# Attention output with both units of a query block in one PSUM bank, normalised between two 32x32 vector transposes

## The chip, the cores and the metric

One NeuronCore of a Trainium2 chip runs the kernel. The metric is device time in microseconds, the median of several executions. One more execution was taken by the hardware profiler. The engines are PE (matmul), ACT (ScalarE), DVE (VectorE), POOL (GpSimd) and SP (which issues the DMAs).

## The reference

`x` has 2 x 1024 tokens of 128 features in float32. The block is FFN, attention, FFN, each with a residual:

```python
x = x + 0.5 * ffn(layernorm(x))      # 8 dense experts of 256 hidden, weighted by norm_g
x = x + attn(layernorm(x))
x = x + 0.5 * ffn(layernorm(x))

# attn: 8 heads of 8 dimensions
xn = (x - mu) * rsqrt(var + eps) * ln_w + ln_b
q, k, v = split(xn @ w_qkv)          # w_qkv 128 x 192
q, k = l2norm(q), l2norm(k)
sim = where(causal, 8.0 * q @ k.T, min)
o = softmax(sim) @ v                 # [b, h, n, 8] -> [b, n, 64]
out = o @ w_out                      # w_out 64 x 128
```

## The kernel before

Tokens are worked in four groups of 512. Group p is (batch p // 2, query block p % 2). Both FFN layers run as rounds of one hidden chunk of 128: three `up` matmuls (L443, L446, L449), a Gelu on ACT, a split into high and low parts on DVE (L932, L934) and three `down` matmuls (L461, L464, L466). PE works LAG = 3 chunks ahead of `down`. Between the two FFN layers lies the attention.

The attention has eight units, numbered u: (batch, query block, quad), a quad being four of the eight heads. A unit of query block 0 has three quad steps, one of query block 1 has seven; that makes 40 quad steps, and units end with steps 2, 5, 12, 19, 22, 25, 32 and 39. A quad step is two steps s, each for two heads: `scores` (L570) writes 2 x up to 512 columns into one of S_SETS = 3 pairs of PSUM banks, and ACT's Exp (L778) moves them to `probs`. The last quad step of each unit is half as wide (256 columns a head). POOL masks the diagonal ones (L1254). `pv` (L591) multiplies `probs` by `v_ones`, whose rows of 32 hold 8 values of a head, a one (which gives the softmax's denominator) and zeros; it accumulates a unit in one bank, 32 partitions a head. `output_bank(u)` alternates between banks 7 and 6.

PE's order is written out: round k has the two `scores` of quad step k, then `pv(k - 3)`, then at most one job of the list `jobs` whose time is k - 3. A job (`fill`) writes the bank that no unit is using, and DVE empties it (`empty`). PE's fill n waits until job n - 1 is emptied, and the first `pv` of a unit waits until every earlier job is emptied. The jobs of one unit's output are:

- `copy_o` on DVE: bank to `oT` (L1076)
- `rows`: four 128x128 transposes of `oT` (L622); DVE then takes the reciprocal (L1107) and multiplies into `o_tok` (L1109)
- after each second unit `features`: four transposes of `o_tok` (L625), copied to `o_feat` (L1114)
- `project`: four matmuls of `o_feat` (64 rows) with `wout_sb` (L628), added to `x_sb` by DVE (L1118)

Other jobs bring in group 3 (LAST): `ln`, `qk`, `v`, `q_stack`, `k_stack` (transposes of groups 2 and 3), and `ffn_ln`, the first transposes of the second FFN. Those of the last unit (`rows`, `features`, `project`) stand in the first group of the second FFN, after chunks 2, 4 and 6; its `copy_o` is at chunk 0 of DVE.

Of the kernel before, what the change touches and what calls it, by code (L numbers as in the profile page):

```python
# [49 lines left out]
ROW = 32  # L50
SCALE = 8.0
# [45 lines left out]
def build(nc, x, ln_w, ln_b, w_qkv, w_out, gate_w, gate_b, rms_w, w1, b1, w2, b2, out):  # L97
# [9 lines left out]
    with ctx:  # L107
# [26 lines left out]
        wout_sb = sb("wout_sb", [INNER, DIM])  # L134
# [35 lines left out]
        oT = sb("oT", [P, GROUP])  # L170
        rden = sb("rden", [P, GROUP_TILES, 4])
        o_tok = sb("o_tok", [P, GROUP_TILES, INNER])
        o_feat = sb("o_feat", [INNER, GROUP])
# [35 lines left out]
        o_copied, rden_done = sem("o_copied"), sem("rden_done")  # L209
# [15 lines left out]
        for st in steps:  # L225
# [10 lines left out]
        u0, u1, u2, u3 = last_quad[0:4]  # L236
        jobs = [(u0 + 1, "rows", 0), (u0 + 2, "q_stack", LAST - 1), (u0 + 3, "k_stack", LAST - 1),
                (u1 + 1, "rows", 1), (u1 + 2, "features", 1), (u1 + 3, "project", 1),
                (u1 + 4, "ln", LAST), (u1 + 5, "qk", LAST), (u1 + 6, "v", LAST), (u2 + 4, "rows", 2),
                (u2 + 5, "q_stack", LAST), (u2 + 6, "k_stack", LAST)]  # L240
        for u in range(3, len(units) - 1):
            at = last_quad[u] + 1
            jobs.append((at, "rows", u))
            if u % 2:
                jobs += [(at + 1, "features", u), (at + 2, "project", u)]
        jobs.append((last_quad[4] + 2, "ffn_ln", 0))
        jobs.sort(key=lambda j: j[0])
        u = len(units) - 1
        jobs += [(quad_steps, "rows", u), (quad_steps, "features", u), (quad_steps, "project", u)]
        assert len({at for at, *_ in jobs}) == len(jobs) - 2  # L250
        job_number = {(kind, arg): n for n, (_, kind, arg) in enumerate(jobs)}

        def output_bank(u):
            return 7 - u % 2

        def job_bank(n):

            at = jobs[n][0]
            return 13 - output_bank(steps[2 * min(at, quad_steps - 1)]["unit"])
# [23 lines left out]
        def schedule(layer, g):  # L283
            if not isinstance(g, int):
                return AT
            return AT_ZERO if (layer, g) == (0, 0) else AT_LAST if (layer, g) == (0, LAST) else AT_THIRD if (layer, g) == (0, 2) else AT_FIRST if (layer, g) == (1, 0) else AT

# [39 lines left out]
        def unit_vectors(eng, p):  # L327
            if p < LAST:
                eng.wait_ge(qkv_copied, p + 1)
            else:  # L330
                eng.wait_ge(job_emptied, job_number["qk", p] + 1)
# [70 lines left out]
        def _(pe):  # L402
# [194 lines left out]
            def fill(n):  # L597
# [3 lines left out]
                if n:  # L601
                    pe.wait_ge(job_emptied, n)
# [677 lines left out]
```

## Time and profile before

| | us |
|---|---|
| median of 3 runs (298.69 to 298.80) | 298.76 |
| the profiled execution | 298.09 |
| its span, first to last instruction | 296.4 |
| first FFN, in the span | 0 to 118 |
| attention | 118 to 194 |
| second FFN | 194 to 296 |

The rows of the trace are in us from the span's start. PE, ACT, DVE and POOL are busy for 280.2, 226.1, 216.8 and 87.0 us of the span. What lies between the span and the execution's time is 298.09 - 296.4 = 1.69 us.

### The profile page before, as it was taken

Reading aid. Unit: us, or ns where it says so; the run is one execution under the profiler, and the core shown is the slowest. Engines: PE = TensorE matmul, PEld = TensorE weight load, DVE = VectorE, ACT = ScalarE, POOL = GpSimd, SP = SyncE. Lnnn points to the kernel's source line nnn. Section 1 sums busy time; section 2 is a strip of 40 time slices with the busy share of each in tenths; the row PEclk is TensorE's granted clock in tenths of the full one; section 3 lists DMA queues with packets and bytes.
Section 4 is the critical chain, followed back from the end, with each engine's and each line's share of the span. In section 5 each row is a group of like instructions: output and inputs, shape, how many; then the busy total and the mean of one; then the engine's idle time right before and its main releaser. Section 6 shows DMA issues by size and latency. Waiting matters only on the chain.

```text
span 296.4 us, 5295 instructions
## 1 busy us (share of the span) xinstructions
PE 280.2 (95%) x1707; PEld 195.6 (66%) x1707; DVE 216.8 (73%) x567; ACT 226.1 (76%) x349; POOL 87.0 (29%) x151
## 2 busy tenths in 40 slices
PE   8898999999989988699989989899999999999995
PEld 8585788788778875143414433268888888888882
DVE  6799988979988886873593451148679797888675
ACT  2875877777877787999798899976677677687672
POOL 5333204204860680542137303212030310310010
PEclk9999999999999999899999999999999999999998
DMA  5710000000000000000000000000000100100101
GB/s 165 237 46 1 0 1 2 0 1 2 0 1 0 3 1 0 2 0 2 0 3 2 1 2 0 2 0 0 2 0 2 35 2 0 35 0 0 35 3 35
DMA packets 8060, 4.66 MB, mean 16 GB/s; under 512 B 642, under 2 KB 8036, under 8 KB 8036
## 3 DMA queue, kind: packets, MB, share of 16 engines
q1 hardware_dynamic: 8036, 4.35, 4.9%
q8 instruction: 13, 0.21, 0.3%
q14 instruction: 11, 0.09, 0.1%
HBM read 3.30 MB, written 1.05 MB: 15 GB/s over the span
## 4 chain that ended last, share of the span: by engine, by line
PE 69%; POOL 9%; ACT 7%; DVE 6%; issue 6%; SPq 1%; DMA 1%; DVEq 0%; POOLq 0%; ACTq 0%
PE ps L591 9%; PE ps L466 8%; PE ps L461 8%; PE ps L443 8%; PE ps L449 8%; PE ps L446 8%; PE ps L464 7%; ACT probs L778 3%; PE ps L570 3%; POOL rstd L1176 2%; PE ps L423 2%; PE ps L628 1%; PE ps L548 1%; PE ps L622 1%; DVE h_lo L934 1%
## 5 line engine op out<-in xcount | busy, mean ns | idle before, releaser
L765 ACT ACTIVATE h<-ps,cols 128x512 f32<-128x512 f32 x128 | 88.0, 690 | 50.5 <-PE ps L449 45.4
L934 DVE TENSOR_TENSOR h_lo<-h,h_hi 128x512 fp32r<-128x512 f32 x128 | 92.0, 724 | 29.0 <-ACT h_hi L768 26.0
L778 ACT ACTIVATE probs<-ps 128x1024 f32<-128x1024 f32 (+1 forms) x80 | 68.6, 962 | 6.1 <-PE ps L570 5.9
L461 PE MATMUL ps<-h_hi,w_hi 128*128 128x512 f32 x128 | 53.0, 414 | 0.3 <-DVE h_hi L932 0.3
L466 PE MATMUL ps<-h_lo,w_hi 128*128 128x512 f32 x128 | 50.9, 398 | 1.8 <-DVE h_lo L934 1.8
L443 PE MATMUL ps<-xT_hi,w_hi 128*128 128x512 f32 (+1 forms) x128 | 50.7, 396 | 0.3 <-ACT xT_hi L839 0.3
L449 PE MATMUL ps<-xT_lo,w_hi 128*128 128x512 f32 (+1 forms) x128 | 50.1, 391 | 0.0
L464 PE MATMUL ps<-h_hi,w_lo 128*128 128x512 f32 x128 | 50.0, 391 | 0.0
L446 PE MATMUL ps<-xT_hi,w_lo 128*128 128x512 f32 (+1 forms) x128 | 49.9, 390 | 0.0
L768 ACT ACTIVATE h_hi<-ps,cols 128x512 fp32r<-128x512 f32 x72 | 49.1, 682 | 0.0
L1254 POOL TENSOR_SCALAR_AFFINE_SELECT probs<-probs 128x256 f32<-128x256 f32 x64 | 26.4, 435 | 54.5 <-ACT probs L778 53.6
L591 PE MATMUL ps<-probs,v_ones 128*32 128x512 f32 (+3 forms) x384 | 40.2, 511 | 0.9 <-DVE x_sb L1118 0.5
L466 PEld LDWEIGHTS ps<-h_lo,w_hi 128*128 128x128 f32 x128 | 24.0, 188 | 9.9 <-DVE h_lo L934 4.8
L932 DVE CAST h_hi<-h 128x512 fp32r<-128x512 f32 x56 | 24.8, 443 | 7.1 <-ACT h L765 6.2
L443 PEld LDWEIGHTS ps<-xT_hi,w_hi 128*128 128x128 f32 x128 | 24.0, 188 | 5.8 <-ACT xT_hi L839 0.5
L461 PEld LDWEIGHTS ps<-h_hi,w_hi 128*128 128x128 f32 x128 | 24.1, 188 | 5.5 <-DVE h_hi L932 1.5
L449 PEld LDWEIGHTS ps<-xT_lo,w_hi 128*128 128x128 f32 x128 | 24.0, 188 | 5.5 <-DVE xT_lo L1129 0.2
L446 PEld LDWEIGHTS ps<-xT_hi,w_lo 128*128 128x128 f32 x128 | 24.0, 188 | 5.1
L464 PEld LDWEIGHTS ps<-h_hi,w_lo 128*128 128x128 f32 x128 | 24.2, 189 | 3.8
L570 PE MATMUL ps<-qT,kT 32*128 32x512 f16 (+3 forms) x192 | 20.0, 335 | 3.5 <-ACT probs L778 3.1
L570 PEld LDWEIGHTS ps<-qT,kT 32*128 32x128 f16 x192 | 5.7, 92 | 20.9 <-ACT probs L778 12.3
L1176 POOL TENSOR_TENSOR gate_rms<-gate_ms,neg_half 128x4 f32<-128x4 f32 x8 | 9.6, 1201 | 29.0 <-DVE gate_ms L899 29.0
(127 smaller groups left out, 301.4 us busy)
## 6 DMA issues: line engine op xcount, KB each, us to landing
w_raw<-in_L_ffn_w SPq DMA_DIRECT2D x8, 256.0 KB, 4.3
x_sb<-in_L_attn_x SPq DMA_DIRECT2D x3, 256.0 KB, 7.3
out_x<-x_sb SPq DMA_DIRECT2D x3, 256.0 KB, 2.3
x_sb<-in_L_attn_x SPq DMA_DIRECT2D x2, 128.0 KB, 2.1
out_x<-x_sb SPq DMA_DIRECT2D x2, 128.0 KB, 1.8
wqkv_sb<-in_L_attn_w_qkv SPq DMA_DIRECT2D x1, 96.0 KB, 6.7
wout_sb<-in_L_attn_w_out SPq DMA_DIRECT2D x1, 32.0 KB, 3.4
small<-in_L_ffn_b SPq DMA_DIRECT2D x1, 8.0 KB
```

Source lines behind the costliest of these rows:

```text
L443: pe.matmul(bank, w1_hi[:, w], xT_hi[:, cols_g], start=True, stop=False)
L446: pe.matmul(bank, w1_lo[:, w], xT_hi[:, cols_g], start=False, stop=False)
L449: pe.matmul(bank, w1_hi[:, w], xT_lo[:, cols_g], start=False, stop=True).then_inc(up_done, 1)
L461: pe.matmul(y, w2_hi[:, w], h_hi[:, c % RING, :], start=(c == 0), stop=False)
L464: pe.matmul(y, w2_lo[:, w], h_hi[:, c % RING, :], start=False, stop=False)
L466: pe.matmul(y, w2_hi[:, w], h_lo[:, c % RING, :], start=False, stop=(c == CHUNKS - 1)).then_inc(down_done, 1)
L570: m = pe.matmul(ps[:, 2 * (s % S_SETS) + hd, at:at + width], kT[rows, st["quad"], k0:k0 + P], qT[rows, st["quad"], qc:qc + width], start=T ...
L591: m = pe.matmul(ps[ROW * j:ROW * j + ROW, bank, q0:q0 + width], v_ones[:, SEQ // P * st["b"] + kt, 4 * st["quad"] + j, :], probs[:, (s + j ...
L765: first = nc.scalar.activation(h[:, slot, :], ps[:, BANK_H + slot, :], ACT.Gelu, bias=bias)
L768: nc.scalar.activation(h_hi[:, slot, :], ps[:, BANK_H + slot, :], ACT.Gelu, bias=bias).then_inc(gelu_done, 1)
L778: nc.scalar.activation(probs[:, s % P_SLOTS, :, 0:width], ps[:, bank:bank + 2, 0:width], ACT.Exp, scale=SCALE).then_inc(exp_done, 1)
L934: dve.tensor_tensor(h_lo[:, slot, :], h[:, slot, :], h_hi[:, slot, :].bitcast(f32), ALU.subtract).then_inc(split_done, 1)
```

## The change

Both units of a query block accumulate in one bank. The weights of quad 0 have their values in rows 0 to 7 and the one in row 8 of the 32; those of quad 1 have them in rows 16 to 23 and 24. So a *pair* of units gives one bank of 128 x 512, and there are four pairs, which end with quad steps 5, 19, 25 and 39. DVE transposes the bank in blocks of 32x32 to `o_blocks`, takes 32 reciprocals a partition, multiplies 256 elements a partition into `o_scaled`, and transposes that in blocks to `o_feat`, which now has 128 rows. `wout_sb` has its 64 rows spread over the same 128, the others zero. There are no `rows` and `features` jobs and no `copy_o`. `qk` and `v` become two `qkv` jobs of two tiles each, `project` becomes two halves except for the last pair, and the order of jobs on PE and of the work around them on DVE is written anew.

```diff
+        first_of_pair = [0] + [quads_until_unit[QUADS * i - 1] for i in range(1, pairs)]
+        q1, q2, q3 = first_of_pair[1:]
+        jobs = [(q1, "ln", LAST), (q1 + 1, "project", (0, 0)), (q1 + 2, "project", (0, 1)),
+                (q1 + 5, "qkv", 0), (q1 + 6, "qkv", 1), (q1 + 7, "q_stack", LAST - 1), (q1 + 8, "k_stack", LAST - 1),
+                (q1 + 12, "q_stack", LAST), (q2 + 1, "k_stack", LAST),
+                (q2 + 4, "project", (1, 0)), (q2 + 5, "project", (1, 1)),
+                (q3 + 1, "project", (2, 0)), (q3 + 2, "project", (2, 1)), (q3 + 5, "ffn_ln", 0),
+                (quad_steps, "project", (pairs - 1, None))]
...
-            sp.dma_start(wout_sb[:, :], w_out).then_inc(wout_in, 16)
+            sp.wait_ge(const_self, 6)
+            for head in range(HEADS):
+                row = ROW * (head % 4) + SPREAD * (head // 4)
+                sp.dma_start(wout_sb[row:row + HEAD_DIM, :], w_out[HEAD_DIM * head:HEAD_DIM * head + HEAD_DIM, :]).then_inc(wout_in, 16)
...
-                if st["first"] and st["unit"] > 1:
+                if opens and pair > 1:
                     pe.wait_ge(job_emptied, sum(at < k for at, *_ in jobs))
...
+                if n == 0 or pair_of_job(n) != pair_of_job(n - 1):
+                    pe.wait_ge(o_copied, pair_of_job(n))
...
                 for half, qkv in qkv_halves(p):
-                    last = nc.scalar.activation(v_ones[:, 4 * p + 2 * half:4 * p + 2 * half + 2, :, 0:HEAD_DIM],
+                    for quad in range(QUADS):
+                        last = nc.scalar.activation(v_of(slice(4 * p + 2 * half, 4 * p + 2 * half + 2), quad),
+                                                    v_columns(qkv, quad), ACT.Copy)
...
                     if layer == 1 and first:
                         if c == 0:
-                            copy_o(len(units) - 1)
-                        if c in (2, 4, 6):
-                            empty(len(jobs) - 4 + c // 2)
-                        if c == 7:
+                            output(pairs - 1)
+                        if c == 3:
+                            empty(len(jobs) - 1)
+                        if c == 4:
                             dve.wait_ge(job_emptied, len(jobs))
...
+            def output(pair):
+
+                dve.wait_ge(pv_done, quads_until_unit[QUADS * pair + QUADS - 1])
+                dve.transpose(o_blocks[:, :, :].rearrange("p b r -> p (b r)"), ps[:, output_bank(pair), :]).then_inc(o_copied, 1)
+                dve.wait_ge(o_copied, pair + 1)
+                split_rows = o_blocks[:, :, :].rearrange("p b (q s) -> p b q s", q=QUADS)
+                dve.reciprocal(rden[:, :, :], split_rows[:, :, :, HEAD_DIM]).then_inc(rden_done, 1)
+                dve.wait_ge(rden_done, pair + 1)
...
+                dve.tensor_tensor(o_scaled[:, :, :].rearrange("p b (q s) -> p b q s", q=QUADS)[:, :, :, 0:HEAD_DIM],
+                                  split_rows[:, :, :, 0:HEAD_DIM],
+                                  rden[:, :, :].unsqueeze(3).to_broadcast([P, BLOCKS, QUADS, HEAD_DIM]),
+                                  ALU.mult).then_inc(o_scaled_done, 1)
+                dve.wait_ge(o_scaled_done, pair + 1)
+                if pair:
+                    dve.wait_ge(job_filled, job_number["project", (pair - 1, 1)] + 1)
+                dve.transpose(o_feat[:, :], o_scaled[:, :, :].rearrange("p b r -> p (b r)")).then_inc(o_ready, 1)
...
-            dve.memset(v_ones[:, 0:TILES // 2, :, HEAD_DIM + 1:ROW].rearrange("p t h r -> p (t h) r"), 0.0).then_inc(v_zero, 1)
+            zero_fill(dve, slice(0, TILES // 2), v_zero)
+            dve.memset(o_scaled[:, :, :].rearrange("p b r -> p (b r)"), 0.0).then_inc(o_zero, 1)
...
+            normalise(ATT, LAST, LAST)
+            for n, (at, kind, arg) in enumerate(jobs[:-1]):
+                if n == 0 or pair_of_job(n) != pair_of_job(n - 1):
+                    output(pair_of_job(n) - 1)
                 if kind == "ffn_ln":
                     normalise(FFN, GROUPS, 0)
                 empty(n)
+                if kind == "ln":
+                    unit_vectors(dve, LAST - 1)
+                if (kind, arg) == ("project", (0, 1)):
+                    stacks(LAST - 1)
+                    dve.wait_ge(job_emptied, n + 1)
+                    first_stats(GROUPS)
+                if (kind, arg) == ("qkv", 1):
                     own_squares(LAST)
                     square_sums(LAST)
+                if (kind, arg) == ("q_stack", LAST - 1):
                     guesses(LAST)
+                if (kind, arg) == ("k_stack", LAST - 1):
                     inverse_lengths(dve, LAST)
                     unit_vectors(dve, LAST)
                     stacks(LAST)
...
+            pool.memset(wout_sb[:, :], 0.0).then_inc(const_self, 1)
+            for quad in range(QUADS):
+                one = SPREAD * quad + HEAD_DIM
+                pool.memset(v_ones[:, :, 4 * quad:4 * quad + 4, one:one + 1], 1.0).then_inc(const_self, 1)
+            zero_fill(pool, slice(TILES // 2, TILES), const_self)
...
-                if s == 3:
+                if s == 5:
                     ln_twice(LAST)
```

q1, q2 and q3 are 6, 20 and 26. `zero_fill` is three memsets where there was one, of the same 1472 columns in all. In the second FFN's first group PE now has one job, `fill(len(jobs) - 1)` after chunk 3. `pair_of_job(n)` is the pair whose quad step the job's time falls in, and `job_bank(n)` is the other pair's bank.

## Rows read from the trace of the kernel before

**Rows 1.** Windows: length, then busy us of PE, PEld, DVE, ACT, POOL; PEclk, DMA, GB/s.

```profile
118.00:124.00 6.00, 3.09 (x31) 1.20 (x30) 4.70 (x21) 5.84 (x12) 2.41 (x8) 1.00 0.00 0
124.00:126.00 2.00, 2.00 (x20) 0.35 (x16) 1.73 (x7) 1.83 (x3) 2.00 (x4) 0.50 0.03 8
181.00:191.00 10.00, 9.30 (x87) 2.54 (x86) 1.24 (x3) 9.96 (x12) 1.09 (x3) 1.00 0.01 2
194.00:290.00 96.00, 96.00 (x471) 78.57 (x462) 75.67 (x190) 69.89 (x114) 13.12 (x13) 1.00 0.03 9
```

**Rows 2.** Waits of ACT from 130 to 194 us: us in total, times, longest.

```profile
ACT probs L778 <- PE ps L570: 5.4, 10, 0.9
```

**Rows 3.** Timeline of ACT: start, us, operation, count, idle before it and what ended it.

```profile
140.64 1.08 ACT L778 ACTIVATE probs<-ps 128x512 f32<-128x512 f32 x2 [0.37 <-PE ps L570]
142.55 1.94 ACT L778 ACTIVATE probs<-ps 128x1024 f32<-128x1024 f32 x2 [0.82 <-PE ps L570]
...
156.60 9.62 ACT L778 ACTIVATE probs<-ps 128x1024 f32<-128x1024 f32 x12 [0.86 <-PE ps L570]
...
181.04 12.09 ACT L778 ACTIVATE probs<-ps 128x1024 f32<-128x1024 f32 x14 [0.24 <-PE ps L570]
```

**Rows 4.** Chain that ended last: start, us, engine, tile, line, count.

```profile
62.59 1.30 PE ps L538 x8
...
118.70 0.34 ACT v_ones L734 x2
...
135.50 0.59 PE ps L622 x4
136.09 0.33 PE ps L570 x4
136.41 0.99 PE ps L591 x8
137.41 0.56 PE ps L625 x4
...
139.29 1.08 PE ps L628 x8
140.38 0.22 PE ps L570 x4
```

**Rows 5.** Timeline of PE: the job behind the third unit's copy.

```profile
155.61 0.63 PE L622 MATMUL ps<-ident,oT 128*128 128x128 f32 x4 [0.44 <-DVE oT L1076]
```

**Rows 6.** Groups of instructions on DVE, forms kept apart: busy us, mean ns, idle before.

```profile
L1076 DVE COPY oT<-ps 128x512 f32<-128x512 f32 x8 | 5.4, 681 | 4.9 <-PE ps L591 4.8
L917 DVE RECIPROCAL logits<-gate_tanh 128x32 f32<-128x32 f32 x8 | 2.8, 353 | 0.3
L1107 DVE RECIPROCAL rden<-ps 128x16 f32<-128x16 f32 x8 | 2.0, 256 | 8.6 <-PE ps L622 8.6
L336 DVE TENSOR_TENSOR qkn<-qk_raw,rnorm 128x256 f32<-128x256 f32 x4 | 1.9, 524 | 0.3
```

**Rows 7.** Chain from 149 us: the vectors and stacks of group 3 on DVE.

```profile
149.46 0.23 DVE newton L311
...
154.24 0.62 DVE k_stack L353
```

**Rows 8.** Chain from 201 us, in the second FFN.

```profile
201.49 0.44 PE ps L622 x4
...
203.75 0.23 PE ps L466
```

**Rows 9.** Timeline of DVE: copy_o of the last unit, and the split behind it.

```profile
200.32 0.67 DVE L1076 COPY oT<-ps 128x512 f32<-128x512 f32 x1
201.46 0.69 DVE L934 TENSOR_TENSOR h_lo<-h,h_hi 128x512 fp32r<-128x512 f32 x1 [0.47 <-ACT h_hi L768]
```

**Rows 10.** Timeline of DVE and of ACT at the start.

```profile
2.91 0.49 DVE L865 BATCH_NORM_STATS2 bn_part<-x_sb 128x6 f32<-128x128 f32 x2 [0.45 <-DMA x_sb<-in_L_attn_x]
6.91 0.63 ACT L830 ACTIVATE w_hi<-w_raw 128x512 fp32r<-128x512 f32 x1 [4.63 <-DMA w_raw<-in_L_ffn_w]
```

More of the change, by code:

```diff
@@ L232, in build @@
         SEED_OPS = 4
[L236 to L250, printed above, removed]
+        pairs = len(units) // QUADS
+        first_of_pair = [0] + [quads_until_unit[QUADS * i - 1] for i in range(1, pairs)]
[6 more added lines that the diff above has]
+                (quad_steps, "project", (pairs - 1, None))]
@@ L261, in vector_rounds, with v_part, v_of @@
+        def v_part(quad):
+            return slice(SPREAD * quad, SPREAD * quad + HEAD_DIM)
+        def v_of(tiles, quad):
+            return v_ones[:, tiles, 4 * quad:4 * quad + 4, v_part(quad)]
         def vector_rounds(layer, c):
@@ L498, in ffn_group @@
                             y_transposes(F - 1, ln_groups=F + 1, att_groups=g - 1 if operands else LAST)
-                    if layer == 1 and first and c in (2, 4, 6):
-                        fill(len(jobs) - 4 + c // 2)
+                    if layer == 1 and first and c == 3:
+                        fill(len(jobs) - 1)
                     if c == at["gate_product"]:
@@ L577, in pv @@
                 st = steps[s]
-                bank = output_bank(st["unit"])
-                if st["first"] and st["unit"] == 0:
+                pair = st["unit"] // QUADS
+                bank = output_bank(pair)
+                opens, closes = st["first"] and st["quad"] == 0, st["last"] and st["quad"] == QUADS - 1
+                if opens and pair == 0:
                     pe.wait_ge(kT_done, LAST - 1)
-                if st["first"] and st["unit"] == 1:
+                if opens and pair == 1:
                     pe.wait_ge(resid, GROUP_TILES * GROUPS)
-                if st["first"] and st["unit"] > 1:
+                if opens and pair > 1:
                     pe.wait_ge(job_emptied, sum(at < k for at, *_ in jobs))
@@ L593, in pv @@
                                       probs[:, (s + j // 2) % P_SLOTS, j % 2, at:at + width],
-                                      start=(st["first"] and n == 0), stop=(st["last"] and n == len(st["item"]) - 1))
+                                      start=(opens and n == 0), stop=(closes and n == len(st["item"]) - 1))
                 m.then_inc(pv_done, 1)
@@ L611, in fill @@
                         m = pe.transpose(bank[:, tile], xn[:, norm, i, :], ident[:, :])
[L612 to L625 removed]
+                elif kind == "qkv":
+                    for i in halves[arg]:
+                        m = pe.matmul(bank[:, 192 * (i % 2):192 * (i % 2) + 192], xf[:, ATT, tiles[i]], wqkv_sb[:, :],
+                                      start=True, stop=True)
                 elif kind == "project":
[L627 removed]
+                    pair, half = arg
+                    pe.wait_ge(o_ready, pair + 1)
+                    for tile in tiles if half is None else [tiles[i] for i in halves[half]]:
                         m = pe.matmul(bank[:, tile], o_feat[:, tile], wout_sb[:, :], start=True, stop=True)
@@ L1158, in _ @@
                     stacks(LAST)
-                if (kind, arg) == ("project", 1):
-                    dve.wait_ge(job_emptied, n + 1)
-                    first_stats(GROUPS)
                 if kind == "ffn_ln":
```

112 lines of the change are left out of this document (44 added, 68 removed).

## The prediction

> **What bounds the kernel now.** I read the windows first, to see which stage has room on which engine. In the second FFN PE is busy for all of 96 us while DVE has 75.67 and ACT 69.89 [rows 1]: there, work taken off PE is time, and work added to DVE costs only where a `down` waits for it. In the attention the picture is different. In the stretch from 181 to 191 us, which has one job in it, ACT is busy for 9.96 of 10 us [rows 1], so Exp sets the pace there. Next I read what ACT waits for. From 130 to 194 us it waits ten times, 5.4 us in all, each time for scores of PE [rows 2]. The reader is to see in this that PE and ACT are nearly balanced, that ACT is the floor, and that 5.4 us is all that lighter PE work can give back there, however much of it is removed.
>
> When does ACT wait? I keep a ledger by round. PE in a full round has scores 0.33 and `pv` 1.00, together 1.33; in a round whose scores are narrow, 0.22 + 1.00 = 1.22 [rows 4]. For ACT, the pair of narrow Exps takes 1.08 [rows 3], with some 0.1 of that beside the next one, so 0.98; fourteen Exps, twelve of them wide, take 12.09 [rows 3], so a full round is (12.09 - 0.98) / 6 = 1.85. A full round thus leaves PE 0.52 for a job, and a narrow round leaves it 0.24 short even without one. Jobs cost PE 0.59 (`rows`, also `ln`), 0.56 (`features`, also a stack) and 1.08 (`project`) [rows 4]. Rounds 9 to 12 have `rows`, `features`, `project` and `ln`, 2.82 in all, and round 12 is narrow. PE needs 3 x 1.33 + 1.22 + 2.82 = 8.03 and ACT 3 x 1.85 + 0.98 = 6.53. PE is short by 1.50, and ACT waits for 0.37 + 0.82 = 1.19 [rows 3]. The 0.31 between them is the lead that the three sets of score banks hold. Round 19, the next narrow one, has a `rows` job of 0.63 that also waits 0.44 for its copy [rows 5]: 1.22 + 0.63 + 0.44 = 2.29 against 0.98, less the lead 1.00, and ACT waits 0.86 [rows 3]. So the ledger holds to 0.15 at both places, and the waits come where jobs meet narrow rounds.
>
> **The change, part by part.** *Attention jobs on PE.* Seven `rows` (0.59 each, 4.1) and three `features` (0.56, 1.7) go. `project` keeps its four tiles, in two halves of 0.54; its weights have 128 rows where they had 64, and I cost that at nothing, because `ln` with 128 rows has the price of the other transposes. `qk` and `v`, eight records each and priced like `project`, become two halves of a product that took 1.30 for four tiles in the first FFN [rows 4], 0.65 each. The jobs now stand in rounds 9, 10, 11, 14, 15, 16, 17, 21, 24, 27, 28, 30, 31 and 34, and none in the narrow rounds 12, 19, 22, 25, 32 and 39. The ledger for rounds 9 to 12 is 5.21 + 0.59 + 0.54 + 0.54 = 6.88 against 6.53: short by 0.35, of which the lead covers 0.31. Rounds 14 to 17: the first is 1.98 against 1.85, short by 0.13; round 15 has a narrow `pv` and is no longer than ACT's; the last two are short by 0.04 each; all inside the lead. Round 19 is short by 0.24, inside the lead too. Rounds 30 to 32 are short by 0.02, 0.02 and 0.24, again inside. So of 5.4 I leave 0.5 for small waits: **4.9 gained**. The least would be what goes with rounds 19 and 12 alone, about 2; the most is 5.4.
>
> *DVE's new chain.* `output` is a transpose, 32 reciprocals, a product of 256 and a transpose. The reciprocal is 0.35 and the product 0.52 [rows 6]. No row shows a block transpose. Below, nothing that reads a bank is under the 0.26 of the reciprocal of 16 [rows 6]; above, I take DVE's slowest stream, the reciprocal, at (353 - 256) / 16 = 6.1 ns an element, 3.1 us for 512. It is nearest to the copy of the same bank to the same kind of tile, 0.68 [rows 6], and I take that: `output` is 0.68 + 0.35 + 0.52 + 0.68 = 2.2. The Trainium skill gives a price in Vector Engine (DVE) Microarchitecture Reference, section 3.8, The reshape front-end and per-opcode configuration: the transpose sustains one element per cycle per lane; no run here shows it yet, and by it the sum is the same.
>
> Who waits for `output`? After pair 0 ends in round 8, `ln` in round 9 (1.85 - 0.59 = 1.3 later) needs only the first transpose, 0.68, and `project` in round 10 (2 x 1.85 - 0.54 = 3.2 later) needs the chain and the emptying of `ln`, a bank read like the copy, 2.2 + 0.7 = 2.9. That is covered with 0.3 to spare. Behind it DVE has the vectors and stacks of group 2 and then the longer chain of group 3, from `qkv` to its stacks, into which the emptying of group 2's stacks is now put. It waits for `k_stack` of group 2 in round 17. From there it has the copy of 0.7 left and, from the first Newton step to the last stack, 154.86 - 149.46 = 5.4 [rows 7], so 6.1; `q_stack` of group 3 is due in round 21, after 3 x 1.85 + 0.98 - 0.56 = 6.0. That is the thinnest place: it has no cover but the lead of 0.3. The pair that opens in round 29 waits for a half of `project` emptied just before, but its scores lie between. I cost all of this at nothing, and the 0.5 kept back above is for it.
>
> *The second FFN.* Two sets of transposes at 0.44 go from PE [rows 8], 0.88 of a stage in which PE never rests. Against this, `output` takes 2.2 at chunk 0 where `copy_o` took 0.67, starting at 200.32; so the split that started at 201.46 [rows 9] starts at about 202.7 and ends at 203.4. The `down` that needs it, L466, was at 203.75 [rows 8], and is now at 203.75 - 0.44 = 203.31. PE waits 0.1, with the semaphore some 0.2; the next split is late by about as much. **Gain 0.6**, between 0 and 0.88.
>
> *Small parts.* ACT has four copies of 64 into `v_ones` instead of two of 128. The last such pair lies on the chain with 0.34 [rows 4]; four take between 0.34 and 0.68, and I add **0.15**. The memset of `o_scaled` and the split ones come before the first statistics, where DVE is idle for 0.45 [rows 10]; 512 columns at no more than the copy's 0.68, with two more starts, push them by 0.2 to 0.4. The work that hides this is the rounding of the first weights, which ACT does at 6.91 after waiting for their DMA [rows 10]: the first features are copied behind it. I cost it at nothing; uncovered it is 0.4. SP's eight DMAs for `w_out` instead of one stand in front of the stores only, which come 100 us after. POOL's `ln_twice` moves behind two more steps of masks, and its reader on DVE then has nothing else until pair 0 ends.
>
> Sum: 4.9 + 0.6 - 0.15 = 5.35. On the profiled execution, 298.09 (its span of 296.4 and 1.69 around it), this gives 292.7; on the median of the runs, 298.76, it gives **293.4**. I predict the median.
>
> **The rivals.** *Half of it is given back.* DVE's order is new and strict: if the stacks of group 3 or `output` come 1 to 2 us later than I count, a fill or a `pv` waits, with every later PE instruction behind it, and ACT runs dry. For it: DVE was the late one in round 19 (0.44 [rows 5]). Against: the covers above. The time is 294.6 to 297.5.
>
> *Slow transposes: slower than before.* With 3.1 us each, `output` is 7.1. `project` in round 10 is then due at 3.2 and ready at 7.8, 4.6 late, less 0.5 of slack in the round; group 3's `k_stack`, which DVE empties behind pair 1's `output`, is due for round 26 and comes some 1 to 2 late; the split in the second FFN ends 4.9 after the new place of its `down`. That is 10 lost against 5.35 gained, 303.5. With t for one transpose the loss in those places is about 4 (t - 0.68), so it decides from t = 2.1. Against it: the copy of the same 512 columns takes 0.68 [rows 6], and what makes the reciprocal slow is its arithmetic, which a transpose lacks.
>
> *The clock falls: slower or equal.* From 118 to 124 us PE is busy for 3.09 of 6 us, and then the granted clock is 0.50 [rows 1], the 1.2 GHz level; 1.00 is the 2.4 GHz level. Less work for PE might do that inside the attention; a full round at the lower level is 2.66 for PE against ACT's 1.85, 0.81 lost, so seven such rounds undo the gain, and twelve make it 293.4 + 9.7 = 303. Against it: from 181 to 191 us, with one job, records cover 9.30 of 10 us and the clock stays at 1.00 [rows 1]; the new jobless rounds look like these. The Trainium skill, TensorE: Matmul & The Clock Gate, Part 1, says that the clock follows how busy PE has recently been, and Part 4 says that transposes do not count for it as other matmuls do; by the first the change could lose the clock, by the second it takes little that counted. The trace agrees with the first and does not show the second.
>
> *Nothing moves in the attention.* If the 5.4 us are the Exps' own pace seen as waits, only 0.45 is left, 298.3. The ledger speaks against it at two places.
>
> **How the numbers follow.** Forecast, 292.4 to 294.6: 0.66. More than that (down to 291.8, small gaps of ACT below the 0.15 that the timeline shows also closing): 0.04. Half given back: 0.20. Slow transposes 0.05, the clock 0.02, nothing moves 0.03. The range of 8 in 10 is 292.0 to 296.4: the forecast's own and most of the given-back case, above which lie the other cases. A measurement of this kernel can tell about 0.2%, 0.6 us, from no change; faster by more than that: 0.90, within: 0.03, slower: 0.07.
>
> **What would show it.** In the profile after: a block transpose near 0.68 and four chains of `output` near 2.2; ACT's waits from 130 us on at 0.5 or less in total; no wait of a fill for `q_stack` in round 21; the last Exp ending some 5 us earlier than at 193.1; one wait of 0.2 or less of PE for L934 in the first group of the second FFN; the clock at 1.00 from 128 us on. The prediction is wrong if a transpose takes over 1 us, if ACT still waits where no job stands, or if DVE's chain passes 2.6 us.

## The result, and the profile after

The changed kernel takes 290.94 us (median of 4 runs, 290.44 to 291.86) against 298.78 us for the kernel before on the same chip (4 runs, 298.69 to 299.05): ratio 0.974, 95% interval 0.971 to 0.977. The profiled execution took 290.44 us, with a span of 288.7 where it was 296.4. The forecast was 293.4 in a range of 292.0 to 296.4: the sign is right and the gain is larger than the range allowed.

The windows of the profile after: length, busy us of PE, PEld, DVE, ACT, POOL, then PEclk. They answer to [rows 1].

```profile
118.00:122.00 4.00, 1.48 (x16) 0.73 (x16) 2.94 (x12) 3.84 (x9) 0.94 (x3) 1.00 0.00 0
122.00:124.00 2.00, 1.53 (x12) 0.38 (x12) 1.83 (x10) 2.00 (x4) 1.80 (x5) 0.94 0.03 8
124.00:126.00 2.00, 2.00 (x20) 0.54 (x20) 1.61 (x7) 1.93 (x3) 1.88 (x4) 0.50 0.00 0
126.00:128.00 2.00, 2.00 (x26) 0.56 (x18) 0.78 (x3) 1.77 (x4) 1.58 (x5) 0.71 0.00 0
128.00:130.00 2.00, 2.00 (x20) 0.59 (x22) 0.00 (x0) 2.00 (x3) 0.81 (x2) 1.00 0.00 0
130.00:186.00 56.00, 53.41 (x540) 18.79 (x536) 28.07 (x70) 55.42 (x67) 19.71 (x47) 1.00 0.01 1
...
188.00:284.00 96.00, 96.00 (x456) 78.37 (x454) 77.44 (x194) 69.65 (x113) 13.12 (x13) 1.00 0.03 9
```

The attention is now a stretch in which ACT is busy for 55.42 of 56 us and the clock stays at 1.00. The second FFN is PE's alone, as before. The timeline of ACT after, which answers to [rows 3]: start, us, operation, count, idle before it.

```profile
127.86 28.48 ACT L794 ACTIVATE probs<-ps 128x512 f32<-128x512 f32 x33
156.70 29.86 ACT L794 ACTIVATE probs<-ps 128x512 f32<-128x512 f32 x36 [0.36 <-PE ps L590]
186.59 1.28 ACT L781 ACT_TABLE_LOAD   x1
```

The reader is to see one wait where there were ten. What PE waited for, as the view of PE's waits after has it (us in total, times, longest), from 118 to 194 us:

```profile
PE ps L590 <- ACT probs L794: 2.9, 5, 0.9
PE ps L497 <- ACT yT L804: 1.4, 1, 1.4
PE ps L568 <- DVE k_stack L370: 0.8, 1, 0.8
```

The first row is healthy: PE waits for ACT to free a set of scores. The third is the one late step of DVE. DVE's new chain after pair 0, in its timeline:

```profile
132.28 0.72 DVE L1091 STREAM_TRANSPOSE o_blocks<-ps 128x512 f32<-128x512 f32 x1 [5.50 <-PE ps L613]
133.03 0.35 DVE L1094 RECIPROCAL rden<-o_blocks 128x32 f32<-128x32 f32 x1
133.42 0.42 DVE L1098 TENSOR_TENSOR o_scaled<-o_blocks,rden 128x256 f32<-128x256 f32 x1
133.88 0.71 DVE L1105 STREAM_TRANSPOSE o_feat<-o_scaled 128x512 f32<-128x512 f32 x1
```

**Where the time went.** I cut both spans at the same events. To the start of the first Exp: 116.60 before, 116.17 after, 0.43 less. From there to the start of the next Exp, with the copies into `v_ones` between: 2.84 and 2.93, 0.09 more. From the start of the pair of narrow Exps at 127.69 before and 127.36 after to the end of the last Exp, 70 Exps in both: 65.43 and 59.20, **6.23 less**. From the first `up` of the second FFN to the last `up` ahead of the gate product, which ends its first group: 17.28 and 16.14, **1.14 less**. The rest differs by under 0.1. Together 7.7.

**How the 6.23 divides.** One more row of the timeline of ACT after, a pair of narrow Exps starting at 161.28 and nine wide ones behind it, gives the pace:

```profile
161.28 9.40 ACT L794 ACTIVATE probs<-ps 128x512 f32<-128x512 f32 x11
```

The starts of wide Exps are 0.903 apart when nothing holds them, those of narrow ones 0.477. The records are longer (1.02 for a wide one that comes after a wait), because the engine starts an Exp before the one ahead of it has ended: 2 x 0.477 + 8 x 0.903 and a last record of 1.22 make the 9.40. At this pace the 70 Exps, 56 of them wide, take 57.5. Before lost 7.9 over that and after loses 1.7. Of the loss before, only 5.6 are shown as idle time of ACT (from 127 us on, small gaps included); after it is 0.6. So 5.0 of the gain was idle time, and 1.2 was time in which ACT is shown as busy. Almost all of the 1.2, 1.1 of it, was lost at the waits themselves, of which there were 13 before, small ones included, and 3 after.

The overlap explains this. A wait shows from the end of one record to the start of the next; but without the wait the next would have started 0.1 to 0.3 ahead of that end. In [rows 3] the pair of 142.55 takes 1.94 and the next starts at 144.96: two starts are 2.41 apart where 1.81 is the pace. Lost are 0.60, and the row shows 0.47.

### The profile page after: what moved, and what is told of

It is laid out like the page before. It is cut to its first block, busy times and chain, and to the rows that moved or that the text cites. A ratio compares the mean times of both kernels' runs of the same rounds, so it can differ in the third digit from the quotient of the medians.

```text
span 288.7 us, 5192 instructions
## 1 busy us (share of the span) xinstructions
PE 274.0 (95%) x1651; PEld 191.0 (66%) x1651; DVE 215.1 (75%) x565; ACT 225.1 (78%) x355; POOL 87.2 (30%) x155
## 4 chain that ended last, share of the span: by engine, by line
PE 71%; POOL 8%; ACT 8%; issue 6%; DVE 4%; SPq 1%; DMA 1%; DVEq 0%; ACTq 0%; POOLq 0%
PE ps L486 9%; PE ps L613 9%; PE ps L463 8%; PE ps L481 8%; PE ps L469 8%; PE ps L466 8%; PE ps L484 8%; ACT probs L794 4%; PE ps L590 4%; PE ps L644 2%; PE ps L443 2%; PE ps L568 2%; POOL rstd L1201 1%; DVE h_lo L950 1%; PE ps L434 1%
## 5 line engine op out<-in xcount | busy, mean ns | idle before, releaser
L794 ACT ACTIVATE probs<-ps 128x1024 f32<-128x1024 f32 (+1 forms) x80 | 67.4, 1002 | 1.0 <-PE ps L590 0.7
L1282 POOL TENSOR_SCALAR_AFFINE_SELECT probs<-probs 128x256 f32<-128x256 f32 x64 | 25.7, 425 | 48.9 <-ACT probs L794 48.3
L590 PE MATMUL ps<-qT,kT 32*128 32x512 f16 (+3 forms) x192 | 20.8, 337 | 3.4 <-ACT probs L794 2.9
L1201 POOL TENSOR_TENSOR gate_rms<-gate_ms,neg_half 128x4 f32<-128x4 f32 x8 | 10.5, 1318 | 28.5 <-DVE gate_ms L915 28.5
```

What stands on the lines that cost most here:

```text
L590: m = pe.matmul(ps[:, 2 * (s % S_SETS) + hd, at:at + width], kT[rows, st["quad"], k0:k0 + P], qT[rows, st["quad"], qc:qc + width], start=T ...
L794: nc.scalar.activation(probs[:, s % P_SLOTS, :, 0:width], ps[:, bank:bank + 2, 0:width], ACT.Exp, scale=SCALE).then_inc(exp_done, 1)
```

## The experiments

Experiments 1 to 4 ran on one chip beside 7 runs of before (median 299.14 us), 5 to 8 beside 13 (299.01), 9 to 12 beside 9 (299.11).

**1. The changed kernel again.** No edit.

> The changed kernel once more, for its spread and a second profile. Its four runs so far lie at 290.4, 290.5, 291.4 and 291.9. All theories: 290.4 to 291.9. If the second level is a lower granted clock for some us after the pause of PE at the start of the attention, a profile at that level shows a longer stretch below 1.00 between 118 and 130 us and the rest alike.

Measured: 291.32 us (291.1 to 291.79), ratio 0.973 (0.972 to 0.975). Its 70 Exps take 59.21 again. Its profiled execution is 1.35 longer than the first. 0.6 of this stands ahead of the first Exp, and 0.75 between 119 and 129 us. Its windows there:

```profile
118.00:122.00 4.00, 1.74 (x17) 0.73 (x16) 2.60 (x9) 3.84 (x12) 0.66 (x2) 0.98 0.00 0
122.00:124.00 2.00, 1.34 (x8) 0.35 (x8) 1.86 (x12) 2.00 (x4) 1.79 (x5) 0.50 0.00 0
124.00:126.00 2.00, 2.00 (x14) 0.33 (x16) 1.58 (x7) 1.72 (x2) 1.83 (x5) 0.50 0.04 8
126.00:128.00 2.00, 2.00 (x24) 0.60 (x16) 1.23 (x4) 1.50 (x2) 1.04 (x4) 0.50 0.00 0
128.00:130.00 2.00, 2.00 (x28) 0.62 (x24) 0.00 (x0) 1.73 (x4) 1.67 (x6) 0.83 0.00 0
```

The granted clock falls to the 1.2 GHz level some 2 us earlier than above, and it is back at the 2.4 GHz level only after 128 us, where above it is back before that. ACT then waits 0.79 before the Exp of 126.50. So two executions of the same program differ by 0.7 in how long PE is at the lower level after its pause at 118 to 122 us. Both kinds occur in executions of before and its variants too: over all fourteen profiled executions the time from the second Exp to the start of the stretch of 70 lies between 8.25 and 9.02.

**2. The old jobs made light.** `rows` and `features` of the kernel before each become one f16 matmul into the same bank, which leaves out what the attention adds to `x`; all waits and DVE's work stay.

```diff
-                    for tile in tiles:
-                        m = pe.transpose(bank[:, tile], oT[:, tile], ident[:, :])
+                    m = pe.matmul(bank, one16[:, 0:P], one16[:, :], start=True, stop=True)
...
-                    for i, tile in enumerate(tiles):
-                        m = pe.transpose(bank[0:INNER, tile], o_tok[:, i, :], ident[:, :])
+                    m = pe.matmul(bank[0:INNER, :], one16[:, 0:INNER], one16[:, :], start=True, stop=True)
```

> The kernel before, with the rows and features jobs each filled by one float16 matmul of 512 columns (about 0.25 us) instead of four transposes (0.56 to 0.59): no output of the attention is computed, all waits, copies and bank handovers stay. Theory A (ledger: ACT waits where PE's round with its job is longer than ACT's round and the lead of 0.3 is used up, and each wait costs another 0.1 because the Exp behind it does not overlap the one in front): ACT's waits after 130 us fall from 5.4 to about 3.2, with restarts and 0.4 in the second FFN 2.9 less in all, about 295.9. Theory B (the gain is in the handovers of banks between PE and DVE, eight before and four after, not in PE's load): 0 to 0.5 less plus 0.4 in the FFN, about 298. Theory C (PE's work sets the attention's time): all of it, 3.8 less, about 295.0.

Measured: 296.36 us (295.92 to 297.19), ratio 0.991 (0.988 to 0.993), 2.8 less. This is theory A's sum, and too far from B's 298, but A's parts are not met: ACT's waits fall to 4.0 and not to 3.2. In the profiles the stretch of 70 Exps takes 63.40, 2.0 less than before, and the first group of the second FFN only 0.1 less, where 0.4 was expected. ACT's timeline, first waits:

```profile
142.34 1.94 ACT L778 ACTIVATE probs<-ps 128x1024 f32<-128x1024 f32 x2 [0.82 <-PE ps L571]
144.75 1.94 ACT L778 ACTIVATE probs<-ps 128x1024 f32<-128x1024 f32 x2 [0.47 <-PE ps L571]
147.11 8.42 ACT L778 ACTIVATE probs<-ps 128x1024 f32<-128x1024 f32 x10 [0.42 <-PE ps L571]
156.15 9.44 ACT L778 ACTIVATE probs<-ps 128x1024 f32<-128x1024 f32 x12 [0.62 <-PE ps L571]
```

Two of the lighter jobs stand in rounds 9 and 10. The wait of 0.37 ahead of the narrow Exps is no longer shown, but the 0.82 behind them is as it was in [rows 3]. What PE gained in rounds 9 and 10 could not help there: `project` in round 11 makes that round 1.33 + 1.08 = 2.41 for PE, against ACT's 1.85, and uses up more than the lead. So lighter jobs give back 2.0 of the 6.2. The rest is further work that went, the places of the jobs, or the four handovers of banks fewer. No run tells these apart: PE's waits for DVE from 128 to 194 us were 1.8 before, in four places, and 0.8 after, in one.

**3. Work put back in full rounds, 4. in narrow rounds.** The changed kernel, with five more sets of four transposes, into the idle bank, in rounds without a job. Both edits differ in the rounds only: 13, 18, 26, 33, 37 (all full), or 12, 19, 25, 32, 39.

```diff
+            def load(at):
+                bank = ps[:, 13 - output_bank(steps[2 * at]["unit"] // QUADS), :]
+                pe.wait_ge(job_emptied, next_job)
+                for i in range(GROUP_TILES):
+                    pe.transpose(bank[:, P * i:P * i + P], ident[:, :], ident[:, :])
...
+                    elif k - PV_LAG in (10, 15, 23, 30, 34):
+                        load(k - PV_LAG)
```

> The changed kernel with four more 128x128 transposes on PE (into the job bank, unused) in five rounds that have full scores and no job (13, 18, 26, 33, 37), 2.8 us of PE work. Theory A: PE's round becomes 1.89 against ACT's 1.85, so 0 to 0.3 more in all. Theory B: 0. Theory C: 2.8 more.

> The same five sets of transposes, 2.8 us of PE work, in the rounds with narrow scores (12, 19, 25, 32, 39). Theory A: each makes PE 0.80 longer than ACT there, less the lead of 0.3, and 0.1 for each new wait of ACT: 2.5 to 3.2 more, five more waits of ACT. Theory B: 0. Theory C: 2.8 more, like the run beside it.

Measured: full 292.48 us (292.15 to 292.79), ratio 0.978 (0.976 to 0.979); narrow 293.55 (293.16 to 294.03), ratio 0.982 (0.980 to 0.983). ACT's timeline, first of the kernel with full rounds, then of the one with narrow rounds:

```profile
128.17 17.17 ACT L802 ACTIVATE probs<-ps 128x512 f32<-128x512 f32 x20 [0.27 <-PE ps L590]
145.57 8.42 ACT L802 ACTIVATE probs<-ps 128x1024 f32<-128x1024 f32 x10 [0.24 <-PE ps L590]
154.21 34.15 ACT L802 ACTIVATE probs<-ps 128x1024 f32<-128x1024 f32 x40 [0.21 <-PE ps L590]
```

```profile
141.76 12.10 ACT L802 ACTIVATE probs<-ps 128x1024 f32<-128x1024 f32 x14 [0.73 <-PE ps L590]
154.24 21.56 ACT L802 ACTIVATE probs<-ps 128x1024 f32<-128x1024 f32 x26 [0.39 <-PE ps L590]
176.45 12.09 ACT L802 ACTIVATE probs<-ps 128x1024 f32<-128x1024 f32 x14 [0.66 <-PE ps L590]
```

The same work costs 1.2 us in full rounds and 2.2 in narrow ones (medians, against the second set of runs of the changed kernel), where 0 to 0.3 and 2.5 to 3.2 were expected. Not all of the 1.0 between them is the narrow rounds' doing. The stretch of 70 Exps is 0.98 longer with full rounds and 1.37 with narrow ones. Another 0.72 comes from the set in round 39, which no scores follow. It stands ahead of the second FFN, where PE alone sets the pace, and the first `up` starts 1.81 behind the last Exp instead of 1.09:

```profile
187.90 0.66 PE L653 MATMUL ps<-ident 128*128 128x128 f32 x4
190.34 0.50 PE L463 MATMUL ps<-xT_hi,w_hi 128*128 128x512 f32 x1
```

The starts of the Exps, taken against the pace, show what a narrow round has to spare. In the changed kernel ACT loses nothing behind rounds 19 and 25, which have a round without a job ahead of them, and 0.37 each behind rounds 12 and 32, which have half a `project` ahead. With a set of transposes in it, round 12 or 32 costs 0.95 and round 19 costs 0.54. So a free round ahead is worth 0.4: that much lead is carried into the narrow one, as the ledger had it with 0.31. Round 25 costs 0.31 with its set; its `pv` is narrow too. In return the loss of 0.58 behind the late `q_stack` of round 21 goes, since DVE has more time with ACT later.

The kernel with full rounds shows the other thing. Of its 0.98 only 0.2 is idle time. About 0.5 is overlap that is lost at waits, seven instead of three, four of them under 0.1 each, and 0.3 is Exps that start when their scores land, a little late, with no idle time shown at all.

**5. The removed work put back in the second FFN.** The changed kernel, with four transposes at chunks 2 and 5 of the first group.

```diff
+                    if layer == 1 and first and c in (2, 5):
+                        pe.wait_ge(job_emptied, len(jobs) - (c == 2))
+                        for i in range(GROUP_TILES):
+                            pe.transpose(ps[:, job_bank(len(jobs) - 1), P * i:P * i + P], ident[:, :], ident[:, :])
```

> The changed kernel with four unused 128x128 transposes put back on PE after chunk 2 and again after chunk 5 of the second FFN's first group, which is the work that the change took from there. If the 1.13 us that this group gained are PE work (0.88 of it transposes, the rest a cheaper project), this run gives 0.88 back, between the first up of the second FFN and its first gate product, and nothing elsewhere. If the gain there was slack of another engine, it gives back 0 to 0.3.

Measured: 291.74 us (291.1 to 292.0), ratio 0.975 (0.973 to 0.978). From the first `up` to the last one ahead of the gate product it takes 16.87, 0.73 more. The median is 0.4 above the second set of runs of the changed kernel, which is inside what the runs differ by. Each set, with the longer starts behind it, takes 0.45, so the two give back 0.90, as was expected. The 0.73 is less because `project`, which now comes later, is 0.16 cheaper here; the next experiment shows why. The transposes are not the whole 1.14.

**6. `project` with 64 rows again.** The changed kernel, with only half of the rows of `o_feat` and `w_out` multiplied (the second quad's heads are left out).

```diff
-                        m = pe.matmul(bank[:, tile], o_feat[:, tile], wout_sb[:, :], start=True, stop=True)
+                        m = pe.matmul(bank[:, tile], o_feat[0:INNER, tile], wout_sb[0:INNER, :], start=True, stop=True)
```

> The changed kernel with project using rows 0 to 63 of o_feat and wout_sb only, so half of the attention's output is left out. The whole project in the second FFN took 1.09 with 64 rows before and 0.89 with 128 rows after. If the number of rows makes the price, it is back at 1.09 here; if the place in the stream does, it stays at 0.89. Either way at most 0.2 in all, plus 0.1 for the halves in the attention.

Measured: 291.38 us (290.62 to 291.81), ratio 0.974 (0.971 to 0.976), the same as the changed kernel. PE's timeline around the `project` of the second FFN, first the changed kernel, then this one:

```profile
195.90 0.39 PE L469 MATMUL ps<-xT_lo,w_hi 128*128 128x512 f32 x1
196.20 1.13 PE L644 MATMUL ps<-wout_sb,o_feat 128*128 128x128 f32 x8
197.09 0.47 PE L481 MATMUL ps<-h_hi,w_hi 128*128 128x512 f32 x1
```

```profile
196.99 0.39 PE L469 MATMUL ps<-xT_lo,w_hi 128*128 128x512 f32 x1
197.34 1.13 PE L644 MATMUL ps<-wout_sb,o_feat 64*128 64x128 f32 x8
198.40 0.50 PE L481 MATMUL ps<-h_hi,w_hi 128*128 128x512 f32 x1
```

From the matmul ahead of it to the one behind it, `project` takes 1.19 with 128 rows and 1.41 with 64, which is also what it took before (207.45 to 208.86 in its timeline). The single records are no longer (272 and 276 ns). The time is lost at the borders: the matmul behind starts 0.20 after the last of `project` with 64 rows, 0.03 after it with 128. Inside the attention the stretch of 70 Exps is 0.2 longer.

The 1.19 is not yet the whole price of 128 rows. `project` in the changed kernel waits a little for DVE, whose transpose into `o_feat` ends at 196.05, behind the start of the matmul ahead; in experiment 5 it ends at 196.89, before that start. There `project` takes 1.04. DVE's last transpose, first in the changed kernel, then in experiment 5, and PE's timeline in experiment 5:

```profile
195.34 0.71 DVE L1105 STREAM_TRANSPOSE o_feat<-o_scaled 128x512 f32<-128x512 f32 x1
...
196.18 0.71 DVE L1109 STREAM_TRANSPOSE o_feat<-o_scaled 128x512 f32<-128x512 f32 x1
```

```profile
197.15 0.39 PE L469 MATMUL ps<-xT_lo,w_hi 128*128 128x512 f32 x1
197.38 1.05 PE L648 MATMUL ps<-wout_sb,o_feat 128*128 128x128 f32 x8
198.19 0.48 PE L481 MATMUL ps<-h_hi,w_hi 128*128 128x512 f32 x1
```

So DVE's chain costs the changed kernel 0.16 in the second FFN.

**7. The kernel before with more instructions at its start.** DVE's one memset of `v_ones` becomes three of the same columns in all, and one of `oT` is added: what the change adds there.

```diff
-            dve.memset(v_ones[:, 0:TILES // 2, :, HEAD_DIM + 1:ROW].rearrange("p t h r -> p (t h) r"), 0.0).then_inc(v_zero, 1)
+            for t0, t1 in ((0, 4), (4, 7), (7, 8)):
+                dve.memset(v_ones[:, t0:t1, :, HEAD_DIM + 1:ROW].rearrange("p t h r -> p (t h) r"), 0.0).then_inc(v_zero, 1)
+            dve.memset(oT[:, :], 0.0).then_inc(o_zero, 1)
```

> The kernel before, with its first memset on DVE cut in three and one of 512 columns behind it, as the change does: three more DVE instructions at the start, no other edit. In the profile before, DVE stood still for 0.32 us at 26.4 us with nothing to wait for, and PE waited 1.4 us for the split behind it; after the change neither is there and the wait is 1.0. If that pause goes with the place of the instructions in DVE's stream, it goes or moves here, and the first FFN ends about 0.4 earlier; if it belongs to something else of the change, it stays, and the time is that of before, 298.8 give or take 0.5.

Measured: 298.66 us (298.29 to 298.92, 10 runs), ratio 0.9986 (0.9973 to 0.9999). DVE's timeline near 26 us, of before and of this kernel:

```profile
26.24 0.17 DVE L899 TENSOR_SCALAR gate_ms<-gate_ms 128x4 f32<-128x4 f32 x1
26.73 1.29 DVE L934 TENSOR_TENSOR h_lo<-h,h_hi 128x512 fp32r<-128x512 f32 x2 [0.32 <-issue]
```

```profile
26.13 0.17 DVE L899 TENSOR_SCALAR gate_ms<-gate_ms 128x4 f32<-128x4 f32 x1
26.21 1.29 DVE L934 TENSOR_TENSOR h_lo<-h,h_hi 128x512 fp32r<-128x512 f32 x2
```

A pause of 0.32 in DVE, which nothing in the profile releases, is gone when instructions are added ahead of it, and PE's wait for L934 goes from 1.4 to 1.0. The first Exp starts at 116.09, 0.5 earlier, and the median is 0.35 below the runs of before beside it, with an interval that reaches almost to no difference. None of the eleven profiles of the changed kernel and its variants has the pause. What it is was not settled.

**8. Every block transpose three times, and 9. twice.** The changed kernel, with the same work repeated. The edit for three (for two, `range(1)`):

```diff
+                for i in range(2):
+                    dve.transpose(o_blocks[:, :, :].rearrange("p b r -> p (b r)"), ps[:, output_bank(pair), :]).then_inc(again, 1)
+                    dve.wait_ge(again, 4 * pair + i + 1)
...
+                for i in range(2):
+                    dve.transpose(o_feat[:, :], o_scaled[:, :, :].rearrange("p b r -> p (b r)")).then_inc(again, 1)
+                    dve.wait_ge(again, 4 * pair + i + 3)
```

> The changed kernel with each block transpose on DVE done three times, one behind the other, so output takes 5.1 us instead of 2.2. By the prediction's count this is just where the gain is gone: project in round 10 comes 2.9 - 0.3 late, less 0.5 of slack, group 3's k_stack 0 to 1 late, and the split in the second FFN 2.9 late: 4.5 to 5.5 more than the changed kernel. If DVE has more room than I counted, 3 more or less.

> Each of the two block transposes of output is made twice: 1.43 more per output, 3.7 instead of 2.3. Three times each cost 12 us, with the granted clock falling behind the waits in rounds 10, 26 and 33. If the cover of an output is about a microsecond (the slack counted ahead of the change was 0.3, and 0.5 in the round), the losses at x2 are under half of those at x3 and the pauses of PE are too short for the clock to fall: 2.5 to 4 us more than the changed kernel. If the clock falls all the same, 6 or more. If the cover is over 1.4 us, nothing.

Measured: three times 303.05 us (300.96 to 304.75), ratio 1.011 (1.006 to 1.017); twice 294.9 us (293.73 to 294.94), ratio 0.985 (0.983 to 0.987). Against the first median of the changed kernel that is 12.1 and 4.0 more, against the second 11.7 and 3.6. For three times, 4.5 to 5.5 were expected. PE's waits from 128 to 192 us, three times:

```profile
PE ps L644 <- DVE o_feat L1111: 2.7, 1, 2.7
PE ps L644 <- DVE xf L1125: 1.8, 1, 1.8
PE ps L590 <- DVE kT L1122: 1.7, 1, 1.7
...
PE ps L568 <- DVE k_stack L370: 0.8, 1, 0.8
```

and its windows around one of them:

```profile
137.00:140.00 3.00, 1.20 (x16) 0.59 (x12) 2.83 (x6) 1.58 (x2) 0.81 (x2) 1.00 0.00 0
140.00:145.00 5.00, 5.00 (x41) 1.58 (x40) 2.35 (x6) 3.02 (x4) 2.40 (x6) 0.66 0.01 3
145.00:150.00 5.00, 5.00 (x52) 2.24 (x48) 2.11 (x12) 4.92 (x6) 0.00 (x0) 1.00 0.00 0
```

Three of the places are those of the rival "slow transposes": `project` in round 10 (1.8), `k_stack` of group 3 (1.7), the second FFN. The longest wait in the attention is at a fourth that neither the rival nor the expectation counted, `project` of pair 2 in round 30, which comes two rounds behind its pair's end like that of pair 0:

```profile
179.99 0.68 PE L644 MATMUL ps<-wout_sb,o_feat 128*128 128x128 f32 x4 [2.70 <-DVE o_feat L1111]
```

The other thing that the expectation lacked is in the windows: PE, busy for 1.20 of 3 us, is then granted less, 0.66 over the next 5 us, and PE catches up more slowly. The same happens behind the waits in rounds 26 and 30, with the lower clock from 168 and from 182 us, but not behind the 2.9 us in the second FFN. With two transposes each the clock stays up (no fall in the records after 128 us) and the loss was in the expected range: in the profiles 0.6 behind round 10, 0.5 behind `q_stack` in round 21, 1.1 behind round 30 and 1.5 in the second FFN. In the second FFN no cover is left at all: PE waits 1.5 and 2.9 for `o_feat` there, for 1.4 and 2.8 added.

**10 to 12. Jobs moved.** The changed kernel, with `q_stack` of group 3 in round 23 instead of 21; that and the second half of `project` of pair 2 in round 33 instead of 31; both and that of pair 0 in round 13 instead of 11, with DVE's stacks of group 2 ahead of its emptying. The last edit in full:

```diff
-        jobs = [(q1, "ln", LAST), (q1 + 1, "project", (0, 0)), (q1 + 2, "project", (0, 1)),
+        jobs = [(q1, "ln", LAST), (q1 + 1, "project", (0, 0)), (q1 + 4, "project", (0, 1)),
...
-                (q1 + 12, "q_stack", LAST), (q2 + 1, "k_stack", LAST),
+                (q2, "q_stack", LAST), (q2 + 1, "k_stack", LAST),
...
-                (q3 + 1, "project", (2, 0)), (q3 + 2, "project", (2, 1)), (q3 + 5, "ffn_ln", 0),
+                (q3 + 1, "project", (2, 0)), (q3 + 4, "project", (2, 1)), (q3 + 5, "ffn_ln", 0),
...
-                if (kind, arg) == ("project", (0, 1)):
+                if (kind, arg) == ("project", (0, 0)):
                     stacks(LAST - 1)
+                if (kind, arg) == ("project", (0, 1)):
```

> Against the changed kernel: the job that transposes q_stack of group 3 stands in round 23 instead of round 21, where PE waited 0.80 for DVE's k_stack and ACT 0.36 behind it. Theory 1 (a wait before an Exp costs what it shows plus the overlap of the two Exps that it breaks, since back-to-back Exps start every 0.903 us): the start after the wait is 1.46 after the one before, so 0.56 is to be had; 0.4 to 0.6 less in the stretch of 69 Exps (59.2), 0.2% of the time. Theory 2 (only the idle time shown counts): 0.36. If the later job makes k_stack or the opening of pair 3 late, nothing is left.

> As q_stack_later, and the second half of project of pair 2 in round 33 instead of round 31, behind the narrow round 32. The wait shown in round 32 is 0.07, its start 0.829 after a narrow Exp where 0.477 is the pace: theory 1 gives another 0.35, so 0.9 in all; theory 2 gives 0.07 more, 0.43 in all.

> As even_jobs, and the second half of project of pair 0 in round 13 instead of round 11, with DVE making the stacks of group 2 before it empties that half. The wait shown in round 12 is 0.15, its start 0.35 late by the pace. Theory 1: 1.26 less than the changed kernel in the Exp stretch, 0.4% of the time; theory 2: 0.58. Against it: the statistics of the second FFN's first group now stand on DVE between that half and the first half of qkv, and may make the fill of the second half late by some tenths.

Measured: 290.95 us (290.8 to 291.1), ratio 0.973 (0.972 to 0.975); 291.63 (291.07 to 291.77), 0.975 (0.973 to 0.976); 291.5 (291.31 to 292.36), 0.976 (0.974 to 0.978). None beats the changed kernel by more than the runs differ. In the first, ACT has no wait that its timeline shows apart:

```profile
127.30 59.79 ACT L794 ACTIVATE probs<-ps 128x1024 f32<-128x1024 f32 x71
```

but its 70 Exps take 58.89, 0.31 less: the loss of 0.56 at 156.70 is gone, but in round 24 an Exp starts 0.30 late with almost no idle time. The number is nearer to theory 2's 0.36 than to theory 1's 0.4 to 0.6, though the loss moved and not merely shrank. In the other two a new wait of 0.32 comes at 179 us, behind `project` in round 33 and `ffn_ln` in round 34, where PE has just come out of a narrow round without lead; their stretch is 0.4 longer than the changed kernel's. Both theories missed there. The third does show what a free round is worth: with round 11 free, the loss behind the narrow round 12 falls from 0.37 to 0.08, but 0.35 and 0.37 come in its place behind rounds 13 and 14. None of the three orders tried is better than that of the changed kernel.

## Why the prediction was right in sign and wrong in size

The profiled execution was forecast at 292.7 and took 290.44, 2.3 less. The attention (1.3 of it) and the second FFN (0.5) are enough to leave the range. By the terms of the sum:

- *Attention, 4.9 forecast, 6.2 measured.* The idle part was right: ACT's idle time fell by 5.0. The step that failed is the claim that "5.4 us is all that lighter PE work can give back there". A wait costs what it shows plus the overlap of two Exps that it breaks, 0.1 to 0.2 each, 1.8 in all over 13 waits before (the small ones included) and 0.7 over 3 after. This makes up 1.1 of the 1.2 by which the gain is larger than the idle time that went. The ledger had the same fault: it took the round of ACT at 1.85 and the narrow pair at 0.98, from the length of records in a row, where the pace is 1.81 and 0.95. [rows 3] held the overlap. The Trainium skill states it in ScalarE: Activation LUTs, What ACT_TABLE_LOAD costs: back-to-back ACTIVATEs overlap by about 93 ns. The trace is near it: 1.02 for a record behind a wait less 0.92 to 0.90 between starts is 0.10 to 0.12 here. In a long row the records grow to 1.23 while the starts stay 0.903 apart, so there the overlap is larger.
- *Where the waits come.* Right in the main: jobs in narrow rounds, and in the round ahead of them (experiments 3, 4 and 12). The lead of 0.31 is real, 0.4 by experiment 4. Still, the ledger had rounds 9 to 12 and 30 to 32 inside it, and behind each of the narrow ones ACT lost 0.37. How much of the gain is lighter work, how much its places, and how much fewer handovers was argued by the ledger and is shown in part only (experiment 2).
- *The prices of jobs.* `project`'s halves took 0.65 (136.31 to 136.96), not 0.54, and half of `qkv` 0.85, not 0.65. Apart from those two losses of 0.37 the slack covered both errors.
- *DVE's chain, 2.2 forecast, 2.3 measured.* The block transpose takes 0.70 to 0.72 from the bank and 0.71 from SBUF, against the copy's 0.68 that was taken for it. The covers held, except at the place named as thinnest: `q_stack` in round 21 was 0.80 late for PE and 0.36 for ACT. In the second FFN `o_feat` came late for `project`, at a cost of 0.16 (experiment 6).
- *The second FFN, 0.6 forecast, 1.14 measured.* The 0.88 for the transposes stands (experiment 5: 0.90). No `down` stalled, so the 0.3 kept back for that was not spent. And `project` became 0.22 cheaper, between its neighbours, by having 128 rows instead of 64, which was "costed at nothing" (experiment 6). 0.88 + 0.22 is 1.10. Without the late `o_feat` it would have been some 1.3, an estimate from these figures.
- *Small parts, 0.15 more forecast, 0.09 measured.* The first FFN was costed at nothing and was 0.43 shorter in this execution. Over eleven profiled executions of the changed kernel and its variants the first Exp starts between 116.11 and 116.82, over three of before and its variants between 116.09 and 116.60, so that is mostly one execution against another, as is how long the clock stays low. A pause of DVE that comes and goes with added instructions may be part of it, 0.35 by the medians of experiment 7, whose interval runs from nothing to 0.8.
- *The rivals.* Half given back did not happen. "Slow transposes" has the right places, and the real price, 0.71, is far from its point of decision. It named 2.1 for this (its own 4 (t - 0.68) reaches 5.35 at 2.0). Between 1.43 and 2.14 per transpose the time goes from 294.9 to 303.05 and passes that of before at about 1.8, if the way between is straight: sooner than was worked out, because round 30 was left out of the count and the clock fell behind three of the long waits. "The clock falls" did not come with lighter work for PE (1.00 from 128 us on), but came with waits of PE. Nothing moves in the attention: refuted.

## What to carry to other kernels

On an engine that runs like instructions back to back, take its pace from the starts of a long unbroken row, multiply by their number, and subtract from the stretch: that is what the stretch can give back. The sum of the waits is too small by the overlap at each, and a stretch with hardly a wait can still lose 1 us: here 1.1 of the 1.7 that were left. And when jobs are spread over rounds, ask of each round whether it has room, and keep the round ahead of a short one free. That gave the short one 0.4 here; room gained further ahead was of no use where a long job stood between.

## What the runs showed of the hardware that was not expected

- An Exp of 128x1024 f32 from PSUM has a record of 1.02 us behind a wait, up to 1.23 in a long row, and starts every 0.903 us; one of 128x512 every 0.477.
- A group of eight f32 matmuls between others of 128 rows takes 1.41 with 64 rows and 1.19 with 128 (1.04 when its input is there in time), at equal length of the records.
- After a stretch in which PE was busy for 1.5 to 1.7 of 4 us, the same program was at the lower clock from 124 to 127 us in one execution and from 122 to 129 us in another, which moves its time by 0.7 us.
- Behind a wait of PE of 1.8 us inside the attention (busy for 1.20 of 3 us) the mean granted clock was 0.66 over the next 5 us. It fell behind two more waits there, of 1.7 and 2.7 us, but not behind one of 2.9 in the second FFN, nor behind the waits of 0.2 to 1.5 with two transposes each.
- DVE made the 32x32 block transposes of 128x512 f32 in 0.71 us, read from PSUM or from SBUF.
